# A mixed attention and FP4 feed-forward kernel: where ScalarE's and VectorE's side jobs stand in TensorE's unit, and a lead of 23 chunks for 22

## The reference

```python
def reference(x, Wq, bq, Wk, bk, Wv, bv, Wo, bo, w_gate, w_up, w_down):
    xn = _layernorm(x, axis=-1)
    return x + attn(xn, Wq, bq, ...) + ffn(xn, w_gate, w_up, w_down)

# attn: 16 heads, D = 8
    scores = jnp.einsum('bhqd,bhkd->bhqk', q, k) * scale + bias[None]
    attn = jax.nn.softmax(scores, axis=-1)
    ctx = jnp.einsum('bhqk,bhkd->bhqd', attn, v)
    return ctx.transpose(0, 2, 1, 3).reshape(B, S, E) @ Wo + bo

# ffn: fp4_linear rounds both operands to FP4 by blocks of 16 first
    h = jax.nn.silu(fp4_linear(x, w_gate)) * fp4_linear(x, w_up)
    return fp4_linear(h, w_down)
```

## Time and profile before

| | |
|---|---|
| median of 3 runs | 903.68 us (900.21 to 904.95) |
| the profiled execution's own time | 894.07 us |
| its span, from first to last instruction | 892.3 us |
| TensorE busy | 772.9 us, 87% |
| VectorE busy | 741.1 us, 83% |
| ScalarE busy | 633.0 us, 71% |
| GpSimd busy | 349.3 us, 39% |
| first score of unit 0 to first score of unit 245 | 66.68 to 848.69 us |

### The profile page before, as it was taken

The page is one execution under the profiler, slowest core; times in us unless marked ns, Lnnn a source line. Parts: engine busy times, 40 slices in busy tenths (PEclk is TensorE's granted clock), DMA queues, the critical chain, the costliest instruction groups (busy, mean ns, idle before and its releaser), DMA issues.

```text
span 892.3 us, 13552 instructions
## 1 busy us (share of the span) xinstructions
PE 772.9 (87%) x4939; PEld 225.7 (25%) x4939; DVE 741.1 (83%) x878; ACT 633.0 (71%) x1262; POOL 349.3 (39%) x271
## 2 busy tenths in 40 slices
PE   3279989898989989897989989898989898979896
PEld 2012223221223323231323323222213231313222
DVE  7898898889888888978898888989897989898920
ACT  4106878777777878776877778777777687767775
POOL 7272172624226373715053553615152505141320
PEclk9557999999999999999999999999999999999999
DMA  5900020131001020320102020310102000000000
GB/s 156 256 13 2 1 72 3 52 92 36 3 13 37 13 72 2 101 44 1 37 2 49 13 73 1 107 37 1 37 2 49 13 3 1 2 1 2 2 1 24
DMA packets 32826, 31.83 MB, mean 36 GB/s; under 512 B 4344, under 2 KB 26552, under 8 KB 32760
## 3 DMA queue, kind: packets, MB, share of 16 engines
q1 hardware_dynamic: 32760, 30.96, 12.8%
HBM read 15.91 MB, written 15.04 MB: 35 GB/s over the span
## 4 chain that ended last, share of the span: by engine, by line
PE 58%; DVE 27%; ACT 8%; issue 4%; POOL 2%; DMA 1%; SPq 0%; ACTq 0%; DVEq 0%; POOLq 0%
PE low L966 22%; DVE neg_max L811 19%; PE mx L936 18%; ACT probs L630 6%; PE low L955 5%; PE mx L1005 3%; PE mx L989 3%; PE low L983 2%; DVE am L784 1%; DVE mb L804 1%; PE low L922 1%; ACT pv_s L667 1%; PE low L997 1%; DVE hid L826 1%; DVE inv L798 1%
## 5 line engine op out<-in xcount | busy, mean ns | idle before, releaser
L811 DVE TENSOR_REDUCE neg_max<-mx 128x1 f32<-128x1024 f32 x512 | 611.6, 1221 | 91.6 <-PE mx L936 80.2
L630 ACT ACTIVATE probs<-low 128x512 f32<-128x512 f32 x1024 | 552.0, 603 | 182.1 <-PE low L955 180.4
L936 PE MATMUL mx<-k_op,q_op 51*128 51x512 bf16 x1024 | 318.5, 398 | 55.9 <-DVE neg_max L811 33.4
L955 PE MATMUL low<-q_op,k_op 53*128 53x512 bf16 x1024 | 329.0, 389 | 8.0 <-ACT probs L630 2.5
L966 PE MATMUL low<-probs,v_op 128*32 128x512 f32 x2048 | 277.4, 614 | 7.1 <-ACT pv_s L667 5.9
L551 POOL TENSOR_SCALAR tanh_s<-tanh_s 128x704 f32<-128x704 f32 x16 | 31.7, 1982 | 313.7 <-ACT gate_s L681 313.7
L936 PEld LDWEIGHTS mx<-k_op,q_op 51*128 51x128 bf16 x1024 | 62.6, 95 | 358.5 <-DVE neg_max L811 197.2
L955 PEld LDWEIGHTS low<-q_op,k_op 53*128 53x128 bf16 x1024 | 68.5, 94 | 76.5 <-ACT probs L630 63.8
L489 POOL TENSOR_SCALAR mb<-mb 128x960 f32<-128x960 f32 (+2 forms) x17 | 58.8, 3456 | 39.6 <-DVE mb L804 37.9
L966 PEld LDWEIGHTS low<-probs,v_op 128*32 128x32 f32 x2048 | 40.5, 108 | 89.9 <-issue 46.1
L477 POOL TENSOR_TENSOR zb<-hid,inv 128x704 f32<-128x704 f32 x16 | 22.2, 1387 | 97.7 <-DVEq L799 97.7
(11 more groups left out here) (120 smaller groups left out, 522.3 us busy)
## 6 DMA issues: line engine op xcount, KB each, us to landing
q_op<-q_rows SPq DMA_DIRECT2D x32, 192.0 KB, 3.8
k_op<-k_rows SPq DMA_DIRECT2D x32, 192.0 KB, 4.7
q_rows<-qp SPq DMA_DIRECT2D x8, 384.0 KB, 2.6
k_rows<-kp SPq DMA_DIRECT2D x8, 384.0 KB, 3.2
x_s<-in_L_attn_inputs_dram SPq DMA_DIRECT2D x8, 256.0 KB, 3.7
q_rows<-qp SPq DMA_DIRECT2D x8, 256.0 KB, 3.1
k_rows<-kp SPq DMA_DIRECT2D x8, 256.0 KB, 3.1
out_dram<-o_s SPq DMA_DIRECT2D x8, 256.0 KB, 2.3
```

What stands on the lines that cost most here:

```text
L630: nc.scalar.activation(probs[U % 3][:, 2 * g + x, :], bank("exp", U, j), ACT.Exp).then_inc(st_free, 1)
L811: nc.vector.tensor_reduce(to, slot("max", pos)[:], AX.X, ALU.max, negate=True).then_inc(mx_free, 1)
L936: ins = nc.tensor.matmul(slot("max", pos)[:, 512 * kh:512 * kh + 512], q, k, start=True, stop=True)
L955: nc.tensor.matmul(bank("exp", U, j), k_op[quad][r, g, kt * P:(kt + 1) * P], q_op[quad][r, g, half * HALF:(half + 1) * HALF], start=True, ...
```

## The change

It does four things.

1. `LEAD` is 23 for 22. By `pos = LEAD + 2 * U + i` the chunk of group 0 now has an odd number, and that of group 1 an even one. The table `HEAD` and the function `chunk` are not changed.
2. The jobs are split. Those that VectorE empties (`middle`) stay between the two groups, and in such a unit the value product moves there too, ahead of them. Those that ScalarE empties (`end`) go to the unit's end, behind the value product. ScalarE takes them after the unit's four exponentials, and `pv_s` after the first exponential for after the second.
3. Some jobs change units: `up` one later; the token groups start 6 later, and their `v` comes 9 units after the start for 3. GpSimd's steps follow by one to two units.
4. VectorE's small steps: the block maxima stand behind the second reduction of their unit for behind the first, the scales and the inverses are parted by a reduction, and the powers come one unit later.

```diff
-LEAD = 22
+LEAD = 23
...
-    return 13 + 60 * (g // 2 - 1) + 15 * (g % 2)
+    return 19 + 60 * (g // 2 - 1) + 15 * (g % 2)
...
-        out += {0: [("xT", p)], 1: [("gate", p, 0)], 2: [("gate", p, 1)], 4: [("up", p)], 12: [("hT", p, 0)],
+        out += {0: [("xT", p)], 1: [("gate", p, 0)], 2: [("gate", p, 1)], 5: [("up", p)], 12: [("hT", p, 0)],
...
-        if 0 <= U - group_unit(g) < 4:
-            out.append((("xnT", "q", "k", "v")[U - group_unit(g)], g))
+        out += {0: [("xnT", g)], 1: [("q", g)], 2: [("k", g)], 9: [("v", g)]}.get(U - group_unit(g), [])
...
+def middle(U):
+
+    return [job for job in extras(U) if job[0] in IN_DVE_RING]
+
+
+def end(U):
+
+    return [job for job in extras(U) if job[0] not in IN_DVE_RING]
...
-                for j in range(2):
+                for j in range(4):
                     exponential(U, j)
-                if U % KT == 1 and U > KT:
...
+                    if j == 0 and U % KT == 1 and U > KT:
...
-                for job in extras(U):
+                for job in end(U):
...
-                        if U == ffn_unit(p) + 5 and i == 0:
+                        if U == ffn_unit(p) + 5 and i == 1:
                             block_maxima(p + 1)
-                        if U == ffn_unit(p) + 5 and i == 1:
-                            block_scales(p + 1)
-                        if U == ffn_unit(p) + 7 and i == 0:
+                        if U == ffn_unit(p) + 6:
+                            (block_scales if i == 0 else block_inverses)(p + 1)
+                        if U == ffn_unit(p) + 8 and i == 0:
                             powers(p + 1)
...
-                    for job in extras(U) if i == 0 else ():
+                    if 0 < U <= NU and i == (0 if middle(U) else 1):
+                        value_product(U - 1)
+                    for job in middle(U) if i == 0 else ():
                         job_on_array(job)
-                if 0 < U <= NU:
-                    value_product(U - 1)
+                for job in end(U):
+                    job_on_array(job)
```

More of the change, by code:

```diff
@@ L150, in rings @@
                     to_act("exp", U, j)
-            for job in extras(U) if i == 0 else ():
-                (to_dve if job[0] in IN_DVE_RING else to_act)(*job)
+            for job in middle(U) if i == 0 else ():
+                to_dve(*job)
+        for job in end(U):
+            to_act(*job)
     return act, dve
@@ L564, in _ @@
                         normalize(g)
-                    if U == group_unit(g) + 2:
+                    if U == group_unit(g) + 4:
                         three_parts(g, 0, "q")
-                    if U == group_unit(g) + 3:
+                    if U == group_unit(g) + 4:
                         three_parts(g, 1, "k")
@@ L571, in _ @@
                         swish(p)
-                    if U == ffn_unit(p) + 5:
+                    if U == ffn_unit(p) + 6:
                         scale_to_grid(p + 1)
-                    if U == ffn_unit(p) + 7:
+                    if U == ffn_unit(p) + 8:
                         round_on_grid(p + 1)
@@ L659, in _ @@
                     act.wait_ge(pv_done, U - 2)
-                for j in range(2):
+                for j in range(4):
                     exponential(U, j)
-                if U % KT == 1 and U > KT:
[L663 to L667, removed]
-                for job in extras(U):
+                    if j == 0 and U % KT == 1 and U > KT:
+                        m = U // KT - 1
+                        act.wait_ge(pv_done, U - 1)
+                        if m:
+                            act.wait_ge(mx_full, MX["pvT", m - 1] + 1)
+                        nc.scalar.copy(pv_s[:], pv).then_inc(pv_kept, 1)
+                for job in end(U):
                     kind, p = job[0], job[1] if len(job) > 1 else 0
@@ L709, in _ @@
                         nc.scalar.copy(dT_s[0:96, 2 * P:3 * P], bank("dT")[0:96, 2 * P:3 * P]).then_inc(st_free, 1)
-                for j in range(2, 4):
-                    exponential(U, j)
         @block.vector
@@ L795, in block_scales, with block_inverses @@
                 mark(nc.vector.tensor_scalar(sc[:, 0:n], am[:, 0:n], 1.0 / 6.0, 1e-12, ALU.mult, ALU.max))
-                link(nc.vector.tensor_scalar(scn[:, 0:n], am[:, 0:n], (1.0 + 2.0 ** -22) / 6.0, 1e-12,
+                mark(nc.vector.tensor_scalar(scn[:, 0:n], am[:, 0:n], (1.0 + 2.0 ** -22) / 6.0, 1e-12,
                                              ALU.mult, ALU.max))
-                link(nc.vector.reciprocal(inv[:, 0:n], scn[:, 0:n]))
-                dve.sem_inc(inv_ok, 1)
+            def block_inverses(job):
+                n = job_cols(job) // BLK
+                settle()
+                nc.vector.reciprocal(inv[:, 0:n], scn[:, 0:n]).then_inc(inv_ok, 1)
             def powers(job):
@@ L872, in _ @@
             block_scales(0)
+            block_inverses(0)
             for pos in range(LEAD):
@@ L880, in _ @@
                     pos = LEAD + 2 * U + i
-                    if i == 1:
-                        for job in extras(U):
-                            job_on_vector(job)
+                    for job in middle(U) if i == 1 else ():
+                        job_on_vector(job)
                     if pos < CHUNKS:
```

## The result

| kernel | median, us | runs | ratio to before, 95% |
|---|---|---|---|
| before | 902.14 (900.21 to 904.95) | 4 | |
| after | 998.94 (994.21 to 1001.95) | 4 | 1.107 (1.101 to 1.112) |

The change makes the kernel 97 us, 10.7%, slower. The profiled execution of after has a span of 999.9 us, against 892.3. Some executions of the kernel before and one of e2 ran at a mean granted clock near 0.93 and took about 2% longer; the medians and ratios leave them out.

A forecast was written before the change was run, and what follows sets the result against it. The bound was taken to alternate between TensorE and VectorE, unit by unit. Terms 11 - 4 - 22 - 9 + 0 + 67 + 4 = +47 on the profiled 894.1 give 941, about 951 as a median, range 908 to 1000.

The forecast's parts named there:

- halves don't matter: Rival: the parity change is free, end jobs gain, middle jobs cost half; -20 us in all, 884; chance 0.05.
- The halves: Each group's four matmuls now share one half of the array, so their starts take 0.88 us for 0.45.
- The first check that I named: In the profile after, a chunk matmul and the score behind it should start 0.21 us apart, not together.
- The unit without jobs: Units with no extra job go from 2.46 to 2.60 us; 78 of them make +11 us.
- VectorE's 2.38, and the trace has 2.46: Before, a unit without jobs was taken as bound by VectorE's two reductions; the 0.08 us above was called VectorE's.
- T = 2.60 + J/2, as long as group 1 can run beside group 0: ScalarE's jobs at the unit's end: a job of length J adds only half of it; -4 us in all.
- matmuls in strict order: Rival: group 1 cannot overtake waiting matmuls, so end jobs add their whole length; 32 us more, 983; chance 0.22.
- Turns: With turn at the unit's end, TensorE's wait for the split maxima goes: -22 us for 31 turns, least nothing.
- The value product: In units with VectorE's jobs it now stands ahead of them and VectorE waits: +67 us, between 45 and 89.
- my last sign of being wrong: The prediction would be wrong if units with `pvT` are no longer than before; 3.25 us forecast, 2.68 before.
- The rival that the maxima come late: Rival: `q_op`'s last rows arrive after the next half's score 0 wants them; 1 us x 31, 982; chance 0.05.
- The rival "faster": Rival: VectorE's backlog hides the value product, so the middle jobs cost nothing; -20 us, 884; chance 0.05.

The follow-up runs named there:

- e2: The kernel before with HEAD turned so that chunk and scores of each group share one half of the array: 1011.96 us, ratio 1.129.
- e6: The kernel before with LEAD 23 and HEAD turned to match, nothing else: 899.69 us, ratio 0.998.
- e5: The changed kernel with halves matched, value product at every unit's end and ScalarE's jobs between the groups again: 898.46 us, ratio 0.997.
- e4: The changed kernel with halves matched by HEAD and the value product at every unit's end again: 909.80 us, ratio 1.013.
- e1: The changed kernel with only HEAD turned, so each group's chunk and scores are in different halves again: 923.77 us, ratio 1.026.
- e10: The kernel before with only the turn jobs moved to the unit's end, behind the value product: 884.42 us, ratio 0.983.
- e12: e5 with the jobs turn and xT alone moved to the unit's end: 888.08 us against before, ratio 0.987.
- e3: The changed kernel, halves still mismatched, with the value product at the end of every unit again: 974.27 us, ratio 1.083.
- e9: The changed kernel with each score ahead of its chunk matmul in group 0 only: 1001.10 us, ratio 1.113.

## Why the prediction was right or wrong

**The forecast and its size.** I said 951 (908 to 1000), slower with a chance of 0.86. It was 998.9: the sign and the range hold, the latter by 1 us, and the loss was twice the +47 of the sum. A path from before to after in single steps puts each part's price beside the sum's terms:

| step | from, to | measured | forecast |
|---|---|---|---|
| lead 23, halves matched | before, e6 | 0 | } -9 |
| moved units, small steps, copy of pv | e6, e5 | -1 | } |
| ScalarE's jobs to the end | e5, e4 | +11 | -46 |
| value product to the middle | e4, e1 | +14 | +34 |
| the mismatch of halves | e1, after | +75 | +67 |

(The forecast column is split as in my rival "halves don't matter": -24 - 22 for the jobs, +34, and 951 less 884 for the mismatch.) The 75 have some clock in them: at a mean clock of 0.962 after has a span of 992.4 and e1 of 922.8, which is 70.

**The halves: right.** Read off and the code, and measured at 67 forecast, 75 found. The first check that I named, chunk and score 0.21 apart, is there (0.23).

**The unit without jobs: near where nothing disturbs it, and its reason wrong.** I forecast 2.60 and the undisturbed one is 2.67. The mean of all 78 is 3.20, though, where the 82 of before have 2.75, so they grew by 0.45 and not by 0.14. Those right behind a job of VectorE's (24 in after, 23 before) have 3.70 for 2.64: the excess that I priced into the jobs falls there. The step "VectorE's 2.38, and the trace has 2.46" waved 0.08 away; it was the sign of the other chain.

**Jobs at the end: the step that failed.** It reads "T = 2.60 + J/2, as long as group 1 can run beside group 0". Group 1 can. This is the gate unit of after:

```profile
490.37 0.40 PE L948 MATMUL mx<-k_op,q_op 51*128 51x512 bf16 x2
490.60 0.38 PE L967 MATMUL low<-q_op,k_op 53*128 53x512 bf16 x1
...
491.72 0.09 PEld L967 LDWEIGHTS low<-q_op,k_op 53*128 53x128 bf16 x1 [0.71 <-ACT probs L641]
491.72 0.39 PE L967 MATMUL low<-q_op,k_op 53*128 53x512 bf16 x1 [0.22 <-ACT probs L641]
492.04 1.06 PE L978 MATMUL low<-probs,v_op 128*32 128x512 f32 x8
...
493.04 0.86 PE L995 MATMUL low<-gT_s,xqT 128*128 128x352 f32 x2
493.83 0.39 PE L948 MATMUL mx<-k_op,q_op 51*128 51x512 bf16 x1
```

The first row is two chunk matmuls in 0.40 us: the first of group 0 and the first of group 1, within 0.02, with three matmuls of group 0 between them in the program. In 19 of the 32 gate units the two start within 0.3. Matmuls of the other half do overtake, three of them. By the Trainium skill ("TensorE: Matmul & The Clock Gate", Part 2) matmuls stay in program order; this trace disagrees, so the rival "matmuls in strict order" had a false mechanism. But its number, 983, was nearer, because its formula T = 2.60 + J is the right one for another reason: score 3 waits for exponential 0 (0.71 in the row), so nothing is gained by group 1 starting early, and the job's 0.79 comes whole on top of 2.67, 3.46. Forecast were 3.00 for `gate`, 2.85 for `hT`, 3.03 for the group jobs; the trace's undisturbed units have 3.46, 3.15 and, for `q`, 3.72. `xT` always follows a `down` here and has 3.35 at the least; by 2.67 + J it is 3.04 for the 2.79 of the sum. With 32 and 32 of them, 16 `xT`, and the 20 group jobs that share their unit with no other job (all taken like `q`), that is some 15 + 10 + 4 + 14 = 43, and 78 x 0.07 = 5 for the units without jobs. The sum lacked 48; that these two make just that is partly chance, since the value product was priced 42 too high, and these are the excesses of undisturbed units; clock and backlogs must make up for it.

**Turns: half to two thirds of the price, and the wrong cause.** -22 forecast, -14 in e10 and, with `xT`, -10 from e5 to e12, where the lead is 23 as in the change. And the cause that I read from the earlier trace rows, the wait for the split maxima, is worth nothing by itself (e6).

**The value product: sign right, too dear.** A `pvT` unit (number 122) in after, forecast at 3.25, takes 3.33 to the next unit's first score, and 3.63 has the unit behind it:

```profile
512.99 0.66 PE L1028 MATMUL mx<-ident,pv_s 128*128 128x128 f32 x4
...
513.87 0.39 PE L948 MATMUL mx<-k_op,q_op 51*128 51x512 bf16 x1 [0.22 <-DVE neg_max L823]
514.01 0.29 DVE L854 TENSOR_TENSOR ctx_s<-mx,pv_r 128x128 f32<-128x128 f32 x1
```

VectorE is at the job while TensorE goes on with group 1, and the next group 0 waits for it, as described. But I had priced the `pvT` unit of before at 2.68 by a sum, and its trace has 3.45 at the least. So my last sign of being wrong came about: units with `pvT` as their only job are shorter in after, 3.44 for 3.85 in the mean (14 and 15 units). The loss is in the unit behind, 3.94 for 2.72; for the two together it is 0.81, with the mismatch in it, where 1.15 was forecast. Taking a quarter off the sum for VectorE's backlog, which I did with little to rest it on, was not enough: 67 forecast in the mismatched kernel, 25 measured (e3).

**Small terms.** The small steps and the copy of `pv` came out at nothing, where I had 0 and -9. The rival that the maxima come late didn't happen: the turns' wait is gone, and no score waits for a DMA among after's long waits. The rival "faster" is disproved by e4 and e1, which lack the mismatch and are still above before.

## What to carry to other kernels

Before a lead, an offset or a loop bound is changed by one, look for what its parity decides; here it decided which half of the array a product uses, and one step cost 75 us, while the edit of the table beside it gives them back. A unit that comes out 0.08 longer than its bound may have another bound: follow the last wait in it, here the third bank, before pricing anything that is placed behind it. And a long job belongs where its engine waits anyway: the gate's 0.79 makes a unit of 2.95 in the middle and of 3.25 or more behind the chain. The best version found is the kernel before with only the short `turn` moved to the unit's end, 884.4 us, 1.7% under before (1.2 to 2.2).

## What the runs showed of the hardware that I had not expected

Matmuls of different halves of the array's rows start out of program order: in after, the first matmul of group 1 starts 0.02 behind that of group 0, ahead of three older ones that wait for their half. The statement at the start that all engines run their queues in order does not hold for TensorE here.

The clock: TensorE is at half clock for 99 us in after and 132 in e9 against 67 in before; in e9 its stretches lie all over the loop, where before has four short ones in it. TensorE's busy share, 91% in both, does not explain it: e3 has 91% too, and 68 us at half clock. What it costs can be estimated from two executions of before, with mean clocks of 0.964 and 0.944 and spans of 893.0 and 904.1: some 37 us more of half clock go with 11 us more of time.
